# Second attention: which engine reads the late items, whose PSUM banks they use, and by how many steps the transposed scores trail

## What is computed

```
Q = x @ wq + bq                      # K, V alike; x is (4, 1024, 256)
Q = Q.reshape(B * H, S, D)           # K, V alike; 16 heads, D = 16, no transpose ahead of it
scores = einsum('bqd,bkd->bqk', Q, K) / sqrt(D)
attn = softmax(scores, axis=-1)
ctx = einsum('bqk,bkd->bqd', attn, V).reshape(B, S, E)
out = ctx @ wo + bo + x              # then a layer norm
```

## Time and profile before

| | us |
|---|---|
| median of 3 runs (2915.7 to 2942.33) | 2937.1 |
| the profiled execution's own time | 2927.07 |
| its span | 2925.5 |
| span in which `group_attention` runs | 1755 to 2590 |
| TensorE busy in 1755 to 2592 | 770.81 |
| VectorE busy in 1755 to 2592 | 671.94 |
| ScalarE busy in 1755 to 2592 | 577.43 |

### The profile page before, as it was taken

The page is one execution under the profiler, slowest core; times in us unless marked ns, Lnnn a source line. Parts: engine busy times, 40 slices in busy tenths (PEclk is TensorE's granted clock), DMA queues, the critical chain, the costliest instruction groups (busy, mean ns, idle before and its releaser), DMA issues. The chain is left out here.

```text
span 2925.5 us, 49732 instructions
## 1 busy us (share of the span) xinstructions
PE 2332.4 (80%) x17258; PEld 1412.3 (48%) x17259; DVE 1681.5 (57%) x2614; ACT 1018.2 (35%) x1925; POOL 357.1 (12%) x431
## 2 busy tenths in 40 slices
PE   3898888753698999999799669899999999945051
PEld 2666666552584555555487553333333333315041
DVE  4776777541242333333266338789888988747842
ACT  2444444211230000000022223667677777731010
POOL 2000000016200000000134420000000000020034
PEclk9999999656799999999999886899999999975576
DMA  6000000135512111111232589454546453021034
GB/s 202 2 0 0 0 0 0 51 125 191 187 43 87 33 35 36 33 35 36 86 101 86 201 236 82 37 50 38 48 36 53 37 48 27 2 67 52 0 115 144
DMA packets 218149, 193.26 MB, mean 66 GB/s; under 512 B 117482, under 2 KB 193938, under 8 KB 215986
## 3 DMA queue, kind: packets, MB, share of 16 engines
q1 hardware_dynamic: 203058, 140.34, 24.8%
q0 software_dynamic: 12672, 34.62, 3.8%
q10 hardware_dynamic: 2304, 16.78, 1.6%
HBM read 109.62 MB, written 81.79 MB: 65 GB/s over the span
## 5 line engine op out<-in xcount | busy, mean ns | idle before, releaser
L1650 DVE TENSOR_REDUCE ga_nmax<-banks 128x1 fp32r<-128x1024 f32 x512 | 621.3, 1221 | 122.6 <-PE banks L1721 121.0
L1680 ACT ACTIVATE ga_probT<-banks 128x512 f32<-128x512 f32 x1024 | 553.8, 597 | 251.6 <-PE banks L1734 207.9
L1721 PE MATMUL banks<-a_ks,a_qs 48*128 48x512 f32 x1024 | 397.8, 476 | 65.3 <-DVE ga_nmax L1650 19.9
L1734 PE MATMUL banks<-a_qs,a_ks 49*128 49x512 f32 x1024 | 392.8, 465 | 7.8 <-DMA a_qs<-ga_max_rows 7.1
L1750 PE MATMUL banks<-ga_probT,a_v 128*32 128x256 f32 (+1 forms) x3840 | 334.6, 422 | 6.2 <-ACT ga_o L1686 6.2
L1721 PEld LDWEIGHTS banks<-a_ks,a_qs 48*128 48x128 f32 x1024 | 166.3, 201 | 289.0 <-DVE ga_nmax L1650 164.3
L1183 PE MATMUL banks<-m_w,rb_xT 128*128 x576 | 288.8, 624 | 0.0
L1030 PE MATMUL banks<-sh_xnT,sh_w 128*128 128x512 f32 x768 | 188.7, 403 | 45.7 <-DVE sh_w L943 23.7
L1165 ACT ACTIVATE rb_silu<-banks 128x512 f32<-128x512 f32 x72 | 43.0, 597 | 516.2 <-PE banks L1183 516.2
L1030 PEld LDWEIGHTS banks<-sh_xnT,sh_w 128*128 128x128 f32 x768 | 148.3, 195 | 82.4 <-issue 52.3
L1734 PEld LDWEIGHTS banks<-a_qs,a_ks 49*128 49x128 f32 x1024 | 161.4, 195 | 29.5 <-ACT ga_probT L1680 19.0
(11 more groups left out here) (288 smaller groups left out, 3479.2 us busy)
## 6 DMA issues: line engine op xcount, KB each, us to landing
sh_xnT<-xnT_parts ACTq DMA_DIRECT2D x16, 1024.0 KB, 4.9
sorted_rows<-wa_zero SPq DMA_DIRECT2D x1, 9216.0 KB, 28.9
rb_xb<-sorted_rows POOLq DMA_DIRECT2D x72, 128.0 KB, 2.3
sorted_out<-rb_yb SPq DMA_DIRECT2D x72, 128.0 KB, 1.7
xnT_parts<-np_parts SPq DMA_DIRECT2D x8, 1024.0 KB, 4.5
m_w<-in_L_ffn_rw_dram SPq DMA_DIRECT2D x2, 4096.0 KB
values<-pg_v SPq DMA_DIRECT2D x16, 512.0 KB, 2.7
a_v<-values SPq DMA_DIRECT2D x16, 512.0 KB, 11.2
```

Source lines behind the costliest of these rows:

```text
L1650: nc.vector.tensor_reduce(nmax[b % 2][:, at:at + 1], slot[:], axis=AX.X, op=ALU.max, negate=True).then_inc(use_read, 1)
L1680: nc.scalar.activation(probT[k % SETS][2 * h + n][:], b_t[w % RING][:], ACT.Exp, scale=SCALE).then_inc(exp_ready, 1)
L1721: return nc.tensor.matmul(slot[:, HALF * kh:HALF * (kh + 1)], qs[a][rows, n, P * q:P * (q + 1)], ks[a][rows, n, HALF * kh:HALF * (kh + 1)] ...
L1734: nc.tensor.matmul(b_t[w % RING][:], ks[a][rows, 2 * gp + n, P * kt:P * (kt + 1)], qs[a][rows, 2 * gp + n, HALF * hf:HALF * (hf + 1)], sta ...
```

## The change

- **Banks.** context, contextT and project leave the two pairs of banks of scores and take the next bank of the ring that scores_T uses (`ring_items`, `place`). Scores alternates between its two pairs, and waits only for the maximum of two steps ago.
- **Readers.** ScalarE reads every bank of the ring, in the ring's order: it copies context to `ctx` (512 columns), contextT as before, and project to `projected` (256 columns). VectorE takes only the reciprocal of the sums, from SBUF. GpSimd multiplies `ctx` by it into `ctxn` and adds `projected` to x.
- **Values.** In all 16 steps of a block weigh is four matmuls of 256 columns.
- **LAG** is UB + 7 = 23 and not UB + 10 = 26. contextT and project stand in the steps j = 10, 13 and 15 of a block's late steps, before 8, 11 and 13, context in 6 as before; j counts from LAG. VectorE's statistics come 5 steps behind the project.

```diff
-    LAG = UB + 10
+    LAG = UB + 7
...
+    STATS_LAG = 5
+    STEPS = UNITS + LAG + UB + STATS_LAG
...
+    def late_items(s):
+        b, j = (s - LAG) // UB - 1, (s - LAG) % UB
+        if not 0 <= b < BLOCKS:
+            return []
+        items = [("context", b)] * (j == 6)
+        if b % 2:
+            items += [("contextT", b // 2)] * (j == 10) + [("project", b - 1)] * (j == 13) + [("project", b)] * (j == 15)
+        return items
+
+    def ring_items(s):
+        back = s - LAG
+        return ([("scoresT", 2 * back), ("scoresT", 2 * back + 1)] if 0 <= back < UNITS else []) + late_items(s)
+
+    place = {item: n for n, item in enumerate(item for s in range(STEPS) for item in ring_items(s))}
...
+            def normalise(b):
+                hf = b % 2
+                src = ctx[hf][:].rearrange("p (q n r) -> p q n r", n=NG, r=BL)
+                pool.wait_ge(rsum_ready, ONE + b + 1)
...
+                nc.gpsimd.tensor_tensor(ctxn[:, :, HQ * hf:HQ * (hf + 1)].rearrange("p n q d -> p q n d"), src[:, :, :, 0:DH],
+                                        rsum[hf][:].unsqueeze(3).broadcast_to([P, HQ, NG, DH]), ALU.mult).then_inc(ctxn_ready, 1)
+
+            def residual(b):
...
+                pool.wait_ge(ring_read, ONE + place["project", b] + 1)
+                nc.gpsimd.tensor_tensor(xt, projected[b % 2][:], xt, ALU.add).then_inc(x_ready, 1)
...
             def outputs(b):
                 act.wait_ge(pv_done, ONE + 2 * RB * (b + 1))
                 if b >= 2:
-                    act.wait_ge(use_done, ONE + use_place["context", b - 2] + 1)
+                    act.wait_ge(ring_done, ONE + place["context", b - 2] + 1)
                 nc.scalar.activation(o[b % 2][:], b_o[:], ACT.Copy).then_inc(o_ready, 1)
 
+            def context(b):
+                at = place["context", b]
+                act.wait_ge(ring_done, ONE + at + 1)
+                if b >= 2:
+                    act.wait_ge(ctxn_ready, ONE + b - 1)
+                nc.scalar.activation(ctx[b % 2][:], b_t[at % RING][:], ACT.Copy).then_inc(ring_read, 1)
...
+            def project(b):
...
+                nc.scalar.activation(projected[b % 2][:], b_t[at % RING][:, 0:D], ACT.Copy).then_inc(ring_read, 1)
...
+            def bank_of(at):
+                if at >= RING:
+                    pe.wait_ge(ring_read, ONE + at - RING + 1)
+                return b_t[at % RING]
...
                 if j == 0 and n == 0:
                     pe.wait_ge(max_in[b % 2], ONE + MAX_IN * (b // 2 + 1))
...
-                    slot_of(use_place["scores", s])
+                    if s >= 2:
+                        pe.wait_ge(max_ready, ONE + s - 1)
                     scores(s, 0)
                 if 0 <= back < UNITS:
-                    scores_T(back, 0)
+                    scores_T(2 * back)
...
-                    if k % RB > 0:
-                        weigh(k, HALF // 2 * (back % 2), HALF // 2)
-                    elif back % 2 == 0:
-                        weigh(k, 0, HALF)
+                    weigh(back // 2 - 2, back % 2)
```

More of the change, by code:

```diff
@@ L1640, in _ @@
             dve.wait_ge(nmax_zero, ONE + 2)
-            for s in range(STEPS):
[L1642 to L1670, removed]
@@ L1672, in _, with weights @@
+            for s in range(STEPS):
+                if s < UNITS:
+                    maximum(s)
+                    if s % UB == UB - 1:
+                        rows(s // UB)
+                for kind, b in late_items(s - 2):
+                    if kind == "context":
+                        inverse(b)
+                for kind, b in late_items(s - STATS_LAG):
+                    if kind == "project":
+                        statistics(b)
         @block.scalar
         def _(act):
[L1674 to L1678, removed]
+            def weights(w):
+                back, n = w // 2, w % 2
+                k, h = back // 2, 1 - back % 2
+                if w % NG == 0 and k >= SETS:
@@ L1695, in _, with context_T @@
[L1695 to L1698, removed]
+            def context(b):
+                at = place["context", b]
+                act.wait_ge(ring_done, ONE + at + 1)
+                if b >= 2:
+                    act.wait_ge(ctxn_ready, ONE + b - 1)
+                nc.scalar.activation(ctx[b % 2][:], b_t[at % RING][:], ACT.Copy).then_inc(ring_read, 1)
+            def context_T(m):
+                at = place["contextT", m]
+                act.wait_ge(ring_done, ONE + at + 1)
+                dst = ctxT[:].rearrange("p h a n t -> p h n a t")
+                src = b_t[at % RING][:].rearrange("p (h n a t) -> p h n a t", h=2, a=A, t=GT)
+                nc.scalar.activation(dst[:, 0], src[:, 0], ACT.Copy)
+                nc.scalar.activation(dst[:, 1], src[:, 1], ACT.Copy).then_inc(ring_read, 1)
@@ new lines, in project @@
+            def project(b):
+                at = place["project", b]
+                act.wait_ge(ring_done, ONE + at + 1)
+                if b >= 2:
+                    act.wait_ge(x_ready, ONE + b - 1)
+                nc.scalar.activation(projected[b % 2][:], b_t[at % RING][:, 0:D], ACT.Copy).then_inc(ring_read, 1)
+            read = {"scoresT": weights, "context": context, "contextT": context_T, "project": project}
+            for s in range(LAG, STEPS):
+                back = s - LAG
+                for kind, arg in ring_items(s):
+                    read[kind](arg)
+                if back % UB == 3 and UB < back < UNITS + UB:
@@ L1750, in weigh @@
                         last = nc.tensor.matmul(b_o[at:at + BL, cols], v[c % SLOTS][:, h, 2 * gp + n, kt, :],
-                                                probT[k % SETS][2 * h + n][:, cols], start=(kt == 0), stop=(kt == RB - 1 and first > 0))
-                last.then_inc(pv_done, 2 * width // HALF)
+                                                probT[k % SETS][2 * h + n][:, cols], start=(kt == 0 and some == 0),
+                                                stop=(kt == RB - 1 and some == 1))
@@ L1774, in project @@
                 for a in range(A):
-                    last = nc.tensor.matmul(slot[:, 0:D], ctxT[:, h, a].rearrange("p n t -> p (n t)"), wo[:, a, :],
+                    last = nc.tensor.matmul(bank[:, 0:D], ctxT[:, b % 2, a].rearrange("p n t -> p (n t)"), wo[:, a, :],
                                             start=(a == 0), stop=(a == A - 1))
-                last.then_inc(use_done, 1)
-            other = {"context": context, "contextT": context_T, "project": project}
+                last.then_inc(ring_done, 1)
@@ L1780, in _ @@
+            late = {"context": context, "contextT": context_T, "project": project}
             for s in range(STEPS):
```

125 lines of the change are left out of this document (62 added, 63 removed).

## The result

The changed kernel takes **3118.58 us** (median of 4 runs, 3116.53 to 3156.04), the kernel before 2931.01 (median of 4). The ratio is 1.0674, with a 95% interval of 1.0577 to 1.077. The profiled run took 3116.53 us, 189 more than that of before. The forecast of 2984 had the sign right and missed by 135 us; the range ended at 3040.

The account below looks back on a forecast made before the run. The prediction held TensorE, VectorE and ScalarE level, TensorE's unit at 1.23 us. The profiled 2927 + 53 (waits and low clock) + 2 (tail) gave 2982 us, 2992 against the median; it forecast 2984, range 2905 to 3040.

Parts of the forecast that it names:

- What bounds the kernel now: Opening section: TensorE, VectorE and ScalarE are level at about 1.2 us a unit; a pair of blocks needs TensorE 43.3 us.
- Item 1: LAG 26 to 23: TensorE waits 2.9 to 3.6 us for the maxima after even blocks, 0 to 0.9 after odd.
- Item 2: Behind each even block's wait the clock falls to 0.50 for some 10.5 us, losing 4.5 us per even block.
- Items 3 and 4: Wait to wait, 24.2 us or 28.7 behind an even block's wait; 769.3 us for 29 blocks against 716.2, +53.
- Item 5: All six waits for keys, and the 3.4 us of pauses per pair of blocks, go; already in the 769.
- Items 6 and 7: ScalarE's added copies, 2.0 us per two blocks, are covered; GpSimd's work is hidden except at the tail, +2 us.
- Item 8: Values in halves: 0.3 us per block, under the wait, so counted as nothing.
- A: Rival: the waits come but the clock does not fall, or seldom; 2915 us (2925 against the median), chance 0.16.
- B: Rival: the maxima are in time, but six waits of 3.5 us for keys come; 2889 us, chance 0.12.
- C: Rival: odd blocks stop too, waiting 3 us, and the clock falls there; 3080 us at most, chance 0.12.
- DMA cost: A fixed cost of about 2.0 us per transfer would make 29 landings some 0.4 us later, 12 us in all.
- shared ports: VectorE and GpSimd share SBUF ports when VectorE reads two SBUF inputs; none kept here does, so nothing was taken.

Follow-up runs that it names:

- lag26_swap: The changed kernel with LAG 26 and the heads of each scores_T pair exchanged, so scores and scores_T read the same half of the partitions; ratio 1.062.
- before_swap: The kernel before with only the heads of scores_T exchanged, so scores and scores_T read the same half of the partitions; ratio 1.104.
- lag23_swap: The changed kernel, LAG 23 kept, with the heads of scores_T exchanged, so scores and scores_T read different halves again; ratio 1.0231.
- before_lag23: The kernel before with LAG 23 and nothing else of the change; ratio 1.083.
- before_halves: The kernel before with the values product of each block's first pair of steps in two groups of 256 columns; ratio 0.9974.
- lag24: The changed kernel with LAG 24 in place of 23, no other edit; ratio 1.0239.
- lag26: The changed kernel with the old LAG 26 in place of 23, no other edit; ratio 0.989.
- lag25_swap: The changed kernel with LAG 25 and the heads of scores_T exchanged, so scores and scores_T keep different halves; ratio 0.9854.

## Why the prediction missed

- **The step that failed** is in "What bounds the kernel now" and goes through all of the sum: "So TensorE's own unit is 1.23 us", read at the end of the function and carried over to LAG 23. That row could not show it. At the tail a unit has no scores any more: it is two scores_T and the values, and after has the same there although its unit is 1.71 (timeline of after, start and length):

```profile
2757.75 0.73 PE L1776 MATMUL banks<-a_qs,a_ks 49*128 49x512 f32 x2
...
2758.98 0.73 PE L1776 MATMUL banks<-a_qs,a_ks 49*128 49x512 f32 x2
```

  So four matmuls side by side on two halves cost before no more than two alone (0.67 against 0.66 us, timeline of before):

```profile
2560.09 0.64 PE L1750 MATMUL banks<-ga_probT,a_v 128*32 128x256 f32 x8
```

  The number read off the tail fitted before for this reason. That it rests on scores and scores_T being on different halves, and so on LAG being even, was not seen. The right number is 1.69 to 1.71 us. It adds 32 x 0.47 = 15.0 us to a pair of 43.3 and makes 58.3. lag26_swap and before_swap show it with nothing but the halves changed, lag23_swap shows it undone, and before_lag23 agrees. Neither this nor its size was among the rivals.
- **Item 1, the wait for the maxima**, vanished because of it. In after TensorE comes to the block's first scores_T 11.64 us behind the end of the block (2005.04 above), by itself:

```profile
2005.28 9.95 SPq L1613 DMA_DIRECT2D a_qs<-ga_max_rows  x16
...
2016.68 0.39 PE L1776 MATMUL banks<-a_qs,a_ks 49*128 49x512 f32 x1
```

  The issues end at 2015.23. With a landing of 1.08 us, as in lag23_swap, the maxima are there at an estimated 2016.31, 0.37 us ahead of it. With the halves right (lag23_swap) it is as forecast, 2.83 to 3.35 (but for one) against 2.9 to 3.6, with a landing of 1.08 us behind the last issue against 1.05, and 0.3 to 0.6 for odd blocks against 0 to 0.9.
- **Item 2, the clock behind the waits**, holds in lag23_swap, but at some 15 us per wait and not the 10.5 assumed. What it lacked is that the clock also stays low with no pause: 1800 to 1925 in after, by estimate some 50 us (from 1811, where before was back at 1.00, 38 units of 3.01 and not 1.70).
- **Items 3 and 4**: 52.9 us per pair forecast, 54.2 in lag23_swap, whose function is 73 us longer than before's against 53 + 2. From the third release to the 32nd block's first scores_T it takes 2639.09 - 1850.99 = 788.1 us where 769.3 was said, which is 14.5 pairs at 1.3 more. The mechanism was right for a kernel that was not the one changed. In the changed one the excess is 182 us, 105 from the unit less what it took away of pauses, and the rest mostly the low clock of the start.
- **Item 5**: the waits for keys are gone in after and in lag23_swap, as said.
- **Items 6 and 7, the readers**: covered, as costed. The 2 us at the tail were not measured by themselves. The new rows of after:

```profile
L1657 POOL TENSOR_TENSOR x<-ga_projected,x 128x256 f32<-128x256 f32 x32 | 23.5, 735 | 202.0 <-ACT ga_projected L1742 202.0
...
L1650 POOL TENSOR_TENSOR ga_ctxn<-ga_ctx,ga_rsum 128x256 f32<-128x256 f32 x32 | 19.9, 621 | 774.1 <-DVE ga_rsum L1685 758.2 <-ACT ga_probT L1714 15.9
...
L1727 ACT ACTIVATE ga_ctx<-banks 128x512 f32<-128x512 f32 x32 | 19.1, 597 | 17.1 <-PE banks L1801 17.1
...
L1742 ACT ACTIVATE ga_projected<-banks 128x256 f32<-128x256 f32 x32 | 12.3, 383 | 34.6 <-PE banks L1817 34.6
```

  ScalarE gets 19.1 + 12.3 = 31.4 us more (some 30 forecast), GpSimd's sum takes 735 ns (732 in the earlier trace rows) and its product 621; TensorE waits for the new readers once, for 1.7 us, at `ga_ctxn`, which only GpSimd's product releases.
- **Item 8**: before_halves, nothing that can be told.
- **Rivals**: A (the clock stays) is refuted by lag23_swap and lag24. B's model holds in lag26, at a ratio of 0.989 against 2889 / 2931 = 0.986. C did not come about: odd blocks stop for 0.6 us at the most in the steady part.
- **The rule on concurrency** would have told it. The Trainium skill, "TensorE: Matmul & The Clock Gate", Part 3, says that small matmuls which sit in different row groups of the array run concurrently. The trace agrees: starts 0.01 us apart on different halves, 0.24 to 0.34 on the same. The rule gives the direction and not the size. For that, the tail of before has two scores_T alone at 0.66 us; four one after the other and the values at 0.57 make an estimate of 1.89 us for the unit, above the 1.71 that came, but far from 1.23. What the prediction drew from the Trainium skill on DMA cost and on shared ports changed nothing. The fixed cost of 2.0 us stands in a section on transfers that GpSimd issues, and these are SyncE's: 0.62 us for an issue (9.95 for 16) and 1.08 from the end of the last one to landing. VectorE's maximum took 1224 ns beside GpSimd's new work and 1221 before.

Two things stay open. One is how long the clock, once at 0.50, stays there. In the kernels with the same halves it is 125 us in after (from 1800) and 100 in lag26_swap (from 1750), with matmuls in flight without a stop; in the later part of before_swap some stretches last 61 us and others 14, in that of before_lag23 61, and 14 or less. Behind the waits of lag23_swap it is 7 to 31 us, behind those of lag24 7 to 34. The other is why before_swap and before_lag23 fall back to it later in the function (71.0 and 65.4 us per pair) while after and lag26_swap don't (58.3, which is the sum at full clock). The first two have their late items in the banks of scores, with short waits for these; no run takes those alone away.

## What to carry to other kernels

When two streams of small matmuls run side by side on the halves of the array, every offset between them (a lag, a ring's length, a moved step) has a parity that belongs to the schedule; write it down beside the constant, and look at start times of neighbouring matmuls in the trace before pricing a shift. A unit's time read off the trace is a property of the order it stands in, so ask what makes it before carrying it over. And shortening a lead by three units bought nothing here. The fastest version, the one with the new banks and readers, LAG 26 and the loads a block earlier, takes 0.971 to 0.975 of the time before, 11% less time in the function's steady part (43.8 us per pair and not 49.2).

## What the chip showed that was not expected

- Two 48- and 49-row matmuls of 512 columns on different halves of the partitions take 0.33 to 0.34 us from start to next start, on the same half 0.56 to 0.58. Two that follow one another at the tail, scores_T alone, take 0.66.
- Behind a pause of 1.77 us in full work (lag24) the granted clock went to 0.50, for some 20 us. Behind one of 1.38 us in lag25_swap, for keys at 2154.82, it did so too, for some 10 us; behind one of 0.85 us in before_halves, at 1872.83, it stayed at 1.00.
- The clock fell in before_swap with no pause of TensorE above 0.63 us in the ten us ahead of it, and stayed at 0.50 with TensorE busy throughout.
- Behind waits of the same kind it differed: behind the wait of 3.19 us that ends at 2038.84 in lag26 the clock was 0.60 to 0.72 for 5 us and then 1.00, while three of its six such waits resumed with matmuls of 0.79 us, those of the low clock.
